# Handing the queries of an attention loop on inside SBUF, in twelve small transfers a unit

## What is computed

```python
qh = q.reshape(b * h, d // h, m)          # h = 8 heads, 32 rows of 512 each
qk = jnp.einsum('bdm,bdn->bmn', qh, kh) * scale
sm = jax.nn.softmax(qk, axis=-1)
ret = jnp.einsum('bmn,bcn->bcm', sm, vh)
```

## Time and profile before

| | |
|---|---|
| median of 3 runs | 1681.23 us (1679.48 to 1682.86) |
| the profiled execution | 1682.86 us, of which its span is 1681.1 us |
| attention loop, first to last `second` | 583.0 to 1078.9 us of the span |
| busy share of the span | TensorE 91%, VectorE 74%, GpSimd 61%, ScalarE 58% |
| DMA queue of SyncE | 94848 packets, 185.88 MB, 38.6% of 16 engines |

### The profile page before, as it was taken

How to read it: one execution, slowest core, us unless ns; L and a number is a source line. 1 busy time by engine, 2 the same in 40 slices (tenths; PEclk the granted TensorE clock), 3 DMA queues, 4 the chain that set the end, 5 groups by cost and what they waited for, 6 DMA issues and landing times.

```text
span 1681.1 us, 28191 instructions
## 1 busy us (share of the span) xinstructions
PE 1531.7 (91%) x8674; PEld 1054.5 (63%) x8674; DVE 1250.4 (74%) x1795; ACT 967.7 (58%) x1523; POOL 1021.2 (61%) x965
## 2 busy tenths in 40 slices
PE   5999999996676599999999999886999999999996
PEld 4677777775442244444444444366998999999985
DVE  7688888888538578888888887245677777777774
ACT  6333333325422167777778777745677676777763
POOL 4788888874203367887787787700355555555553
PEclk9999999998789589999999999987999999999998
DMA  6344444427452847677776764292244444444443
GB/s 248 114 139 139 143 140 142 137 102 202 100 154 72 194 118 191 184 181 190 189 184 180 197 186 133 70 331 102 51 76 76 76 79 81 80 76 76 76 77 50
DMA packets 110842, 224.24 MB, mean 133 GB/s; under 512 B 12704, under 2 KB 12704, under 8 KB 109856
## 3 DMA queue, kind: packets, MB, share of 16 engines
q1 hardware_dynamic: 94848, 185.88, 38.6%
q0 software_dynamic: 15904, 37.23, 12.7%
HBM read 146.71 MB, written 75.84 MB: 132 GB/s over the span
## 4 chain that ended last, share of the span: by engine, by line
PE 36%; DMA 23%; issue 3%; DVE 2%; ACT 1%; POOL 1%; SPq 0%; POOLq 0%; DVEq 0%; ACTq 0%
DMA out_rows<-XN,slots 21%; PE pB L1377 10%; PE pA L1359 8%; PE pO L1387 8%; PE pO L1400 4%; PE pO L1538 1%; DMA XN<-normed_rows,slots 1%; PE pO L1510 1%; PE pA L1527 1%; PE pB L1368 1%; PE pA L1449 1%; POOL out_rows L1343 1%; PE pB L1475 1%; PE pA L1456 1%; DVE low L1710 1%
## 5 line engine op out<-in xcount | busy, mean ns | idle before, releaser
L1710 DVE TENSOR_REDUCE low<-pA 128x2 f32<-128x1024 f32 x256 | 306.7, 1219 | 86.5 <-PE pA L1359 77.0
L1608 ACT ACTIVATE pt<-pB 128x512 f32<-128x512 f32 x512 | 290.0, 593 | 105.3 <-PE pB L1377 102.9
L430 PE MATMUL y<-kv,toep 128*128 128x288 f32 x1280 | 327.8, 413 | 9.0 <-DVEq L63 5.8
L1343 POOL DMA_INDIRECT out_rows<-XN,slots x71 | 196.8, 2772 | 216.0 <-DMA out_rows<-XN,slots 166.3
L430 PEld LDWEIGHTS y<-kv,toep 128*128 128x128 f32 x1280 | 239.1, 191 | 97.5 <-DVEq L63 34.1
L1527 PEld LDWEIGHTS pA<-XN,fc 128*128 128x128 f32 x2272 | 267.2, 193 | 7.7 <-ACT fc L1667 1.2
L1527 PE MATMUL pA<-XN,fc 128*128 128x128 f32 x2272 | 267.9, 277 | 1.7 <-DVE XN L1871 1.7
L1377 PE MATMUL pB<-qs,ks 98*128 98x512 f32 x512 | 229.1, 451 | 2.7 <-ACT pt L1608 2.4
L1377 PEld LDWEIGHTS pB<-qs,ks 98*128 98x128 f32 x512 | 97.0, 191 | 186.8 <-ACT pt L1608 121.9
L1359 PE MATMUL pA<-ks,qs 96*128 96x512 f32 x512 | 196.2, 428 | 19.5 <-DMA qs<-q_low 17.3
L400 ACT ACTIVATE ym<-y 128x384 f32<-128x384 f32 (+1 forms) x128 | 52.5, 410 | 230.7 <-PE y L430 230.7
(11 more groups left out here) (262 smaller groups left out, 2443.6 us busy)
## 6 DMA issues: line engine op xcount, KB each, us to landing
ks<-ctx_high SPq DMA_DIRECT2D x64, 256.0 KB, 5.0
qs<-q_high SPq DMA_DIRECT2D x64, 256.0 KB, 7.0
kc<-in_ctx_conv SPq DMA_DIRECT2D x32, 384.0 KB, 5.5
XN<-in_x SPq DMA_DIRECT2D x16, 512.0 KB, 9.8
toep<-kernel_and_skip SPq DMA_DIRECT2D x32, 256.0 KB, 3.5
ct<-in_ctx SPq DMA_DIRECT2D x16, 512.0 KB, 6.7
ctx_high<-kh SPq DMA_DIRECT2D x16, 512.0 KB, 4.4
ctx_low<-kl SPq DMA_DIRECT2D x16, 512.0 KB, 5.2
```

Source lines behind the costliest of these rows:

```text
L430: m = pe.matmul(y[half].rearrange("p (l n) c -> p l n c", l=CB)[:, l, :, 0:PAIRS], toep[u][:, (l - s) * P:(l - s + 1) * P], kv[u][:, half, ...
L1343: pool.indirect_dma_start(out=out["out"], out_offset=bass.IndirectOffsetOnAxis(ap=slots[:, j:j + 1], axis=0), in_=ys[j % 2], in_offset=Non ...
L1608: act.activation(pt[s][:, h, :], bank(u, n), ACT.Exp, scale=SCALE1).then_inc(s_exp, 1)
L1710: dve.tensor_reduce(ap(low[u % 2], t % CB * NH + t // CB, [[NH, 2], [1, 1]]), pA[n % 2], op=ALU.max, axis=AX.X, negate=True).then_inc(s_re ...
```

## The change

The queries no longer pass through DRAM. The two stores (`store_query`) and their semaphore `s_qs` are gone, and so are the three query loads of 256 KB. In their place SyncE copies `nexth`, `nexth` and `nextl` straight from SBUF to the three thirds of `qs`. A source of 128 partitions can't be folded into 32 partitions x 4 heads in one transfer here, so there are three transfers for each head, twelve of 64 KB a unit. Units 0 to 3 keep the six loads (`load_first`).

The timing of the pieces moves too. ScalarE makes `nextq` after exp 13 and `nexth` after exp 14; VectorE makes `nextl` in the next body after reduce 3; SyncE waits for `nextl` behind the three key loads, and only then comes to the twelve transfers and to `shift`. `nexth` may be written again when the twelve have landed, so ScalarE waits for the load's semaphore `s_ld` at `nexth`.

```diff
+        LATER = 3 + 3 * NH
+        def loaded(i):
+            return 16 * LATER * i + 16 * LOADS
...
-            def store_query(j):
+            def load_next(j, u):
+                load(j, u)
                 sp.wait_ge(s_ql, j - 3)
-                sp.dma_start(QHr[j], nexth).then_inc(s_qs, 16)
-                sp.dma_start(QLr[j], nextl).then_inc(s_qs, 16)
+                for h in range(NH):
+                    head = slice(h * HD1, (h + 1) * HD1)
+                    for dst, src in ((qs[u][0:HD1, h], nexth), (qs[u][HD1:2 * HD1, h], nexth), (qs[u][2 * HD1:NS, h], nextl)):
+                        sp.dma_start(dst, src[head]).then_inc(s_ld[u], 16)
...
                         sp.wait_ge(s_b, made(j - 1, place(j - 1, CB - 1, NH - 1)))
-                        sp.sem_inc(s_go, 1)
-                        sp.wait_ge(s_qs, 32 * j)
-                    load(j + 3, n)
+                        load_next(j + 3, n)
+                    else:
+                        load_first(j + 3, n)
                 if exists(j + 1):
                     shift(j + 1, (u + 1) % TRIP)
-                if exists(j + 4):
-                    store_query(j + 4)
...
-            def query_high(j):
+            def query_high(j, i, u):
                 act.wait_ge(s_q, 2 * j - 7)
-                wait(act, s_qs, 32 * j - 128)
+                if not isinstance(j, int) or j > 4:
+                    act.wait_ge(s_ld[(u + 3) % TRIP], loaded(i + (u + 3) // TRIP))
...
-                        if NH * s + h == 1 and exists(j + 4):
-                            query(j + 4)
-                        if NH * s + h == 5 and exists(j + 4):
-                            query_high(j + 4)
...
+                        if NH * s + h == TURN + 3 and exists(j + 4):
+                            query(j + 4)
+                        if NH * s + h == TURN + 4 and exists(j + 4):
+                            query_high(j + 4, i, u)
...
-                    if beat == 9 and exists(j + 4):
-                        query_low(j + 4)
+                    if beat == 3 and exists(j - 1) and exists(j + 3):
+                        query_low(j + 3)
```

More of the change, by code:

```diff
@@ L1034, in _build @@
         s_st = [sem(f"s_st6{i}", st) for i in range(4)]
-        (s_one, s_a, s_red, s_sp, s_b, s_exp, s_md, s_add, s_sum, s_av, s_ln, s_inv, s_att, s_x3, s_go, s_bn, s_mv, s_q, s_ql, s_qs) = [
+        (s_one, s_a, s_red, s_sp, s_b, s_exp, s_md, s_add, s_sum, s_av, s_ln, s_inv, s_att, s_x3, s_go, s_bn, s_mv, s_q, s_ql) = [
             sem(n + "_6", st) for n in ("s_one", "s_a", "s_red", "s_sp", "s_b", "s_exp", "s_md", "s_add", "s_sum",
-                                        "s_av", "s_ln", "s_inv", "s_att", "s_x3", "s_go", "s_bn", "s_mv", "s_q", "s_ql", "s_qs")]
+                                        "s_av", "s_ln", "s_inv", "s_att", "s_x3", "s_go", "s_bn", "s_mv", "s_q", "s_ql")]
         G = 8
@@ L1109, in _build @@
         LOADS = 6
+        LATER = 3 + 3 * NH
         units = lambda d: d.rearrange("b (g h d) c -> (b g) d h c", g=TH, h=NH)
         KHu, KLu, QHu, QLu = units(KH), units(KL), units(QH), units(QL)
-        QHr, QLr = (d.rearrange("b (th p) c -> (b th) p c", p=P) for d in (QH, QL))
         def unit_loop(eng, body):
@@ L1156, in load, with load_first @@
             def load(j, u):
-                for dst, src in ((ks[u][0:HD1], KHu[j]), (ks[u][HD1:2 * HD1], KLu[j]), (ks[u][2 * HD1:NS], KHu[j]),
-                                 (qs[u][0:HD1], QHu[j]), (qs[u][HD1:2 * HD1], QHu[j]), (qs[u][2 * HD1:NS], QLu[j])):
+                for dst, src in ((ks[u][0:HD1], KHu[j]), (ks[u][HD1:2 * HD1], KLu[j]), (ks[u][2 * HD1:NS], KHu[j])):
                     sp.dma_start(dst, src).then_inc(s_ld[u], 16)
-            def store_query(j):
+            def load_first(j, u):
+                load(j, u)
+                for dst, src in ((qs[u][0:HD1], QHu[j]), (qs[u][HD1:2 * HD1], QHu[j]), (qs[u][2 * HD1:NS], QLu[j])):
+                    sp.dma_start(dst, src).then_inc(s_ld[u], 16)
+            def load_next(j, u):
+                load(j, u)
                 sp.wait_ge(s_ql, j - 3)
-                sp.dma_start(QHr[j], nexth).then_inc(s_qs, 16)
-                sp.dma_start(QLr[j], nextl).then_inc(s_qs, 16)
+                for h in range(NH):
+                    head = slice(h * HD1, (h + 1) * HD1)
+                    for dst, src in ((qs[u][0:HD1, h], nexth), (qs[u][HD1:2 * HD1, h], nexth), (qs[u][2 * HD1:NS, h], nextl)):
+                        sp.dma_start(dst, src[head]).then_inc(s_ld[u], 16)
             def load_values(j, u):
@@ L1205, in _ @@
             for u in range(3):
-                load(u, u)
+                load_first(u, u)
                 load_values(u, u)
@@ L1354, in score @@
                 if t == 0:
-                    pe.wait_ge(s_ld[u], 16 * LOADS * i + 16 * LOADS)
+                    pe.wait_ge(s_ld[u], loaded(i))
                 if half == 0:
```

## The result

The changed kernel takes 1688.86 us (median of 6), the kernel before 1680.89 in the same series: ratio 1.0053, 95% interval 1.0029 to 1.0078. The forecast was 1688.0. That the total fits so well is partly luck, as the experiments show: an ordinary unit lost less than I had forecast, and the copies, which I had at nothing, cost something.

A forecast was written before the change was run, and what follows sets the result against it. TensorE was taken to bound the kernel, so only its delays count. A unit becomes 8.98 + 0.69 + 6.14 = 15.81 us against 15.56; in all 6.8 us more, 1688.0 us from the median, range 1675 to 1696.

The forecast's parts named there:

- nextl's slot ahead of reduce 7: VectorE, beat 3: nextl's slot of 0.61 us delays reduce 7 and so score 10, a loss of 0.55 us a unit.
- the gain of taking `nextl` from beat 9: VectorE, beat 9: without nextl reduce 11 is ready for score 14, whose wait goes; a gain of 0.31 us a unit.
- GpSimd's lock: VectorE, beat 3: nextl might wait for a small GpSimd instruction, 0.26 us more a unit; taken as not happening; rival's chance 0.07.
- ScalarE at nothing: ScalarE: nextq and nexth moved to beats 13 and 14 are hidden by values groups, 0.36 us spare; no cost.
- DRAM trip at nothing: DMA: two stores and three loads of 256 KB replaced by twelve 64 KB copies, transfers hidden before and after; no cost.
- SyncE at nothing, with 1.5 us to spare: SyncE: twelve issues 0.48 us apart, then shift, landed by 14.2 us against 15.81 needed; all hidden.
- rival 4: SyncE: copies late, issues 0.65 us apart or landing after 5 us, so shift lands late; 12 or 31 us more; chance 0.08.
- The landing of the last copy: SyncE: last of the twelve copies, issued at 10.8 us, lands at about 13.4 us, before nexth wants it at 14.87.
- Sum: Whole kernel: 26 units lose 0.25 us each, 6.5 us; with units 1 and 28, 6.8 us more.
- Unit 1: Loop's unit 1: it has no measure, so reduce 7 has room; a gain of 0.2 us.
- unit 28: Late unit that gets a nextl it did not have, and its own late reduce 7; a loss of 0.5 us.
- A bound that was none: Loop: unit 29, without the moved work, takes 15.33 us, said to limit any move's gain to 0.23 us a unit.

The follow-up runs named there:

- e2: Changed kernel with a second, equal-sized subtraction on zeros behind nextl on VectorE; unit 16.31 us, median 1701.68 us, ratio 1.0108 to the kernel before.
- e8: Kernel before with nextl made at beat 7, after reduce 7, instead of beat 9; unit 15.19 us, median 1668.10 us, ratio 0.9935.
- e4: Changed kernel with the queries through DRAM again, the engines' new order kept; unit 15.71 us, median 1684.98 us, ratio 1.0019 to the kernel before.
- e9: Changed kernel with queries through DRAM again and nextl at beat 7 instead of 3; unit 15.18 us, ratio 0.9942 to the kernel before.
- e3: Changed kernel with two more 64 KB copies of zeros between the twelve and shift; unit 16.82 us, ratio 1.0289 to the kernel before.
- e10: Changed kernel, twelve copies kept, with nextl at beat 7 instead of beat 3; unit 22.03 us, 1884.41 us in one run.

## Why the prediction was right, step by step

*nextl's slot ahead of reduce 7.* Right in mechanism and place. Forecast slot 0.61, measured 0.60; score 10 at 8.98 us, measured 817.12 - 808.24 = 8.88; second 10 to the next opening 6.14, measured 823.96 - 817.81 = 6.15. e2 doubles it and gets the double. The unit is 15.72 where I had 15.81, because reduce 3 starts 3.39 us into the unit and not 3.48. In the kernel before, reduce 15 still carried part of the lateness of beat 9 into score 2 of the next unit: the pair of scores 1 and 2 takes 0.73 us in unit 14 of the kernel before (first line) and 0.63 in that of the changed one.

```profile
804.07 0.73 PE L1359 MATMUL pA<-ks,qs 96*128 96x512 f32 x2
809.04 0.63 PE L1368 MATMUL pA<-ks,qs 96*128 96x512 f32 x2
```

I had looked for the gain of taking `nextl` from beat 9 only at score 14, and so made that term too small. The experiments give both terms. Leaving beat 9 is worth 15.57 - 15.19 = 0.38 us (e8), where I had 0.31; standing ahead of reduce 7 costs 15.71 - 15.18 = 0.53 (e4 and e9), where I had 0.55. Their difference is the 0.15 measured, where I had 0.25.

*GpSimd's lock.* I took the meeting with a small instruction as not happening, without any margin. It did happen, but in the other direction: GpSimd waited (0.68 us), which cost nothing.

*ScalarE at nothing.* Right (e9 against e8).

*DRAM trip at nothing.* Right: e4 and the changed kernel have the same ordinary unit.

*SyncE at nothing, with 1.5 us to spare.* Wrong, and hidden by the total. I took the spacing of the copies from stores to DRAM, 0.48, though the one issue in the trace that moves data inside SBUF, `shift` itself, was 0.65 apart. I had it as rival 4 with 0.08. It cost 2.0 us of the loop's 6.5 (e4) and left 0.17 us of spare (e3). The spacing came out as rival 4 had it, 0.63; what kept `shift` from binding in every unit is that it released TensorE 2.0 us after its issue and not the 2.3 that I had taken from the stores. Rival 4 also names a section of the Trainium skill ("DMA: Bandwidth & Descriptors", section "Anatomy of one DMA — SWDGE (gpsimd) path"); that section is on transfers issued by GpSimd, and these are SyncE's. The landing of the last copy was wrong too: I had it at 13.4 us, ahead of `nexth` at 14.87, and in unit 1 `nexth` waited for it until 15.33.

*Sum.* I had 6.8 us for the slot and 0 for the copies. The loop shows 4.5 and 2.0. That the 0.10 us a unit too much for the slot and the 2.0 us of the copies nearly cancel is luck. Unit 1, which I had gaining 0.2, gains that only in e4, because the copies took it back; unit 28 lost 16.10 - 15.47 = 0.63, forecast 0.5. Unit 0, forecast as untouched, took 0.44 less (17.67 us; it takes 17.6 to 18.2 over the runs). The medians are 8.0 us apart, 1.5 more than the loops.

*A bound that was none.* I called unit 29's 15.33 us the least that any move could give. e8's loop runs at 15.19. The written-out units are a likeness, not a floor: in e8 units 1, 2, 3 and 29, which stand outside the hardware loop, take 15.33 to 15.34 as well. Against a unit of the loop, unit 29 takes 0.06 us more from second 2 to second 3 and 0.08 more from second 9 to second 10; why, no run shows.

## What to carry to other kernels

Before adding an instruction to a queue, find the stretch of that queue with no gap in it and the wait that its end feeds; a slot there costs its length in full, and the same instruction one place later, behind the stretch, may cost nothing. An instruction that can't run beside another engine's wants to be issued just ahead of a seam in that engine's work: here that was worth 0.37 us a unit (e8), while taking the queries' trip through DRAM away gave an ordinary unit nothing. And many small transfers ahead of a short urgent one cost it the sum of their issues, even when every byte is hidden. An engine's busy time doesn't tell its slack: GpSimd looked 3 us free in a unit, and 1.3 us more made it the bound.

## What the runs showed of the hardware

- Issuing a transfer from SBUF to SBUF took SyncE 0.59 us at the median for the copies of 64 KB and 0.61 for the 8 KB of `shift` in the changed kernel; by kind of transfer, those with DRAM on one side took 0.34 to 0.43 at the median in the kernel before. A copy of 64 KB landed 2.0 us after its issue at the median, 3.0 at most.
- VectorE's subtraction of two SBUF tiles and GpSimd's instructions kept each other waiting, one whole instruction at a time and in both directions, and the waiting one gets in even between two instructions 0.07 us apart: `nextl` took 2.65, 1.80 or 0.68 us depending on what GpSimd had begun. VectorE's reduces, which read PSUM, kept their 1.2 us beside GpSimd's additions. The Trainium skill ("SBUF — State Buffer", section "Who interferes with whom") says that issue order decides who blocks; all three lengths, and GpSimd's 0.68 instead of 0.27, agree.
- After 5.05 us of idle TensorE's granted clock was 0.50 of full for the next 3.56 us (e10), so a long wait cost more than its own length.
